# Computing the expert gates of a vision tower inside its second attention, and storing the normalised rows beside the balancing

## The reference, cut to what matters

```python
h = _layernorm(h + _L1_attn_ref(h, ...))     # causal attention in each image, 8 heads, mixed with a moving average
h = _layernorm(h + _L1_ffn_ref(h, gate_w, experts))

def _L1_ffn_ref(x, gate_w, experts):         # e = 8 experts
    gates = x @ gate_w                       # [64 images, 65 tokens, 8]
    cg = sinkhorn(gates)                     # 8 rounds: normalise over tokens, then over experts
    vals, idx = top_k(cg per expert, m)      # m = 65 // 8 = 8 rows per expert, of all 4160
    gate_values = (vals > 0.5)
    outputs = (x[idx] @ experts) * gate_values
    return (sum of the outputs that fell on a row) / (their count + 1)

def _layernorm(x, eps=1e-05):
    return (x - mean(x)) / sqrt(var(x) + eps)
```

## Time and profile before

| | us |
|---|---|
| median of 3 runs | 896.49 |
| the profiled execution | 896.61 |
| its span, first to last instruction | 894.8 |

### The profile page before, as it was taken

One profiled execution on the slowest core, in us unless ns is written; L12 is line 12 of the kernel. 1 busy time (PEld: TensorE's weight loads), 2 busy tenths in 40 slices (PEclk: granted clock), 3 DMA queues, 4 the chain that ended last, 5 costly groups with the idle time before them and its releaser, 6 DMA issues. The chain is left out here.

```text
span 894.8 us, 21478 instructions
## 1 busy us (share of the span) xinstructions
PE 655.1 (73%) x8452; PEld 529.1 (59%) x8452; DVE 526.6 (59%) x948; ACT 328.2 (37%) x774; POOL 245.0 (27%) x283
## 2 busy tenths in 40 slices
PE   2999999999999966507877787696877777455002
PEld 2888888888888854407625565585666566354001
DVE  0365666666655663362125778686778888333862
ACT  0113444434444443304422343433666767411000
POOL 0353334443333330000012233202443443252000
PEclk9999999999999976555698878555999999555555
DMA  8523343222222000159204300000000000033000
GB/s 330 214 111 120 139 158 127 108 108 108 108 108 108 2 2 1 45 147 155 42 0 51 46 0 0 1 0 2 2 2 0 0 1 3 1 98 94 24 1 4
DMA packets 32913, 57.45 MB, mean 64 GB/s; under 512 B 12370, under 2 KB 29954, under 8 KB 30370
## 3 DMA queue, kind: packets, MB, share of 16 engines
q1 hardware_dynamic: 32803, 56.74, 21.5%
q0 software_dynamic: 64, 0.07, 0.0%
HBM read 48.14 MB, written 8.66 MB: 63 GB/s over the span
## 5 line engine op out<-in xcount | busy, mean ns | idle before, releaser
L375 PE MATMUL a_bank<-a_x,a_tok_w 128*128 128x256 f32 (+1 forms) x608 | 150.4, 389 | 15.8 <-DVE a_ht L555 15.8
L375 PEld LDWEIGHTS a_bank<-a_x,a_tok_w 128*128 128x128 f32 (+1 forms) x608 | 113.0, 192 | 37.3 <-DMA tables<-in_tables 15.7
L124 POOL TENSOR_TENSOR a_qt<-a_qp,data 128x512 f32<-128x512 f32 x64 | 71.9, 1155 | 2.1 <-POOL a_qp L616 1.6
L616 POOL TENSOR_TENSOR a_qp<-a_rope 128x260 f32<-128x260 f32 x16 | 11.8, 734 | 177.2 <-DVE a_rope L499 177.2
L282 ACT ACTIVATE a_at<-a_bank 65x256 f32<-65x256 f32 x128 | 38.9, 390 | 25.9 <-PE a_bank L259 25.9
L1340 ACT ACTIVATE b_at<-b_bank 65x512 f32<-65x512 f32 x64 | 34.9, 601 | 36.5 <-PE b_bank L1214 36.5
L493 DVE SCALAR_TENSOR_TENSOR a_ht<-a_bank,data 128x256 f32<-128x256 f32 x16 | 7.7, 484 | 64.4 <-PE a_bank L375 64.4
L259 PE MATMUL a_bank<-a_mix,a_e 64*65 64x64 f32 x1024 | 40.6, 234 | 0.0
L1403 POOL TENSOR_TENSOR b_e<-b_e,b_inv 128x520 f32<-128x520 f32 (+1 forms) x32 | 35.5, 1110 | 13.8 <-DVE b_inv L1278 13.7
L259 PEld LDWEIGHTS a_bank<-a_mix,a_e 64*65 64x65 f32 x1024 | 36.0, 147 | 4.0 <-issue 3.4
L172 DVE TENSOR_REDUCE a_mx<-a_bank 128x6 f32<-128x390 f32 (+1 forms) x48 | 25.6, 534 | 21.1 <-PE a_bank L146 21.1
(11 more groups left out here) (241 smaller groups left out, 1536.0 us busy)
## 6 DMA issues: line engine op xcount, KB each, us to landing
a_x<-in_x SPq DMA_DIRECT2D x16, 2304.0 KB, 7.9
lag_rows<-r_kernel SPq DMA_DIRECT2D x1, 4192.5 KB, 39.4
lags<-lag_rows SPq DMA_DIRECT2D x1, 2112.5 KB
base<-places SPq DMA_DIRECT2D x1, 2080.0 KB
token_rows<-n_h SPq DMA_DIRECT2D x16, 130.0 KB
out<-n_plain SPq DMA_DIRECT2D x16, 130.0 KB
expert_weights<-in_w SPq DMA_DIRECT2D x2, 1024.0 KB, 5.8
a_tok_w<-in_tok_w SPq DMA_DIRECT2D x1, 1152.0 KB, 6.7
```

The costliest lines, as they stand in the source:

```text
L124: nc.gpsimd.tensor_tensor(qt[:, b * BLOCKS * P:(b + 1) * BLOCKS * P].rearrange("p (c h i) -> p c h i", i=qb, h=HEADS), wide(by_image[:, b, ...
L375: mm = nc.tensor.matmul(banks[0][:, 0:GP], w[0:rows, k * DIM:(k + 1) * DIM], x[p][0:rows, k * GP:(k + 1) * GP], start=(k == 0), stop=(k == ...
```

## The change

The gates are computed in the attention's loop from `z`, the row before its mean is subtracted and before it is scaled. The mean is taken out of the gate matrix instead (once, at the head of the block, with one matmul), and the scale `rstd` is multiplied into the 65x512 gates at the head of the last block. In the loop that adds, per group, four transposes and four matmuls on TensorE (each fp32 matmul shows as two records) and two copies on ScalarE; the mean's scaling moves from VectorE to ScalarE. `output` waits for the copy of the gates of the group before, since both share a bank.

The orders of the engines in that loop are rearranged: TensorE turns the last token's rows with the first half and makes the values before the second half; VectorE takes the first maxima ahead of the first subtraction, and `residual` and the row sums before both inversions; the last token's rows (`LAST`) are in the first part of the exponentials; ScalarE saves heads before it squares, and squares one group later.

`norm_and_gate` is gone. Its head stands in the last block, `norm_and_route`. ScalarE makes the plain rows with one instruction per image beside the balancing, and SyncE stores them. The table of `h3` rows is gone too: the 64 rows are gathered from the output, together with the standard deviations of the second norm by a second indirect DMA, and multiplied by them on VectorE.

```diff
-        LAST = PAIRS * UNIT
+        LAST = UNIT
+        FIRST = (0, UNIT + 1)
...
+        parts = [slice(0, UNIT + 1), slice(UNIT + 1, SLOTS)]
...
-                wait_past(pe, S.z_ready, g)
+                wait_past(pe, S.gates_saved, g)
...
+            def turn_rows(g):
+
+                pe.wait_ge(S.z_ready, g + 1)
+                for b in range(GI):
+                    mm = nc.tensor.transpose(ybank[:, b * TOKENS:(b + 1) * TOKENS], z[:, b, :], T("ident", TOKENS)[:, 0:TOKENS])
+                mm.then_inc(S.z_turned, 1)
+
+            def gates(g):
+                pe.wait_ge(S.zf_ready, g + 1)
+                for b in range(GI):
+                    mm = nc.tensor.matmul(gatebank[:, b * EXPERTS1:(b + 1) * EXPERTS1], zf[:, b * TOKENS:(b + 1) * TOKENS],
+                                          gate[:, :], start=True, stop=True)
+                mm.then_inc(S.gates_done, 1)
+
+            nc.tensor.matmul(banks[2][:, 0:EXPERTS1], T("mean"), D("gate1"), start=True, stop=True).then_inc(S.gate_mean, 1)
+            pe.wait_ge(S.gate_ready, 1)
...
                     turn_pair(g, p, 0)
+                    turn_last(g, p)
                 if exists(g + 2):
                     if exists(g + 1):

                         pe.wait_ge(S.masked, 2 * (g + 2))
                     queries_keys(g + 2)
+                if exists(g + 1):
+
+                    pe.wait_ge(S.masked, 2 * (g + 2))
+                    values(g + 1, 1 - p)
                 if exists(g):
-                    turn_last(g, p)
+                    pe.wait_ge(S.probs_ready, 2 * g + 2)

                     pe.wait_ge(S.at_ready, 5 * g + 2)
                     turn_pair(g, p, 1)
@@ -1238,14 +1264,14 @@
                     pe.wait_ge(S.v_ready, g + 1)
                     values_of_image(nc, 0, at, vs[p], obank)
                     values_of_image(nc, 1, at, vs[p], obank)
-                if exists(g + 1):
-
-                    pe.wait_ge(S.masked, 2 * (g + 2))
-                    values(g + 1, 1 - p)
+                if exists(g - 1):
+                    turn_rows(g - 1)
                 if exists(g):
                     pe.wait_ge(S.at_ready, 5 * g + 5)
                     values_of_image(nc, 2, at, vs[p], obank)
                     values_of_image(nc, 3, at, vs[p], obank).then_inc(S.av_done, 1)
+                if exists(g - 1):
+                    gates(g - 1)
...
-            def average(g):
+            def total_of_rows(g):
                 dve.wait_ge(S.z_ready, g + 1)
+
+                wait_past(dve, S.mean_scaled, g)
                 nc.vector.tensor_reduce(sums[:, :], z[:, :, :], AX.X, ALU.add).then_inc(S.sum_done, 1)
-                dve.wait_ge(S.sum_done, g + 1)
-                nc.vector.tensor_scalar(means[:, :], sums[:, :], 1.0 / DIM, None, ALU.mult).then_inc(S.mean_scaled, 1)

             nc.vector.tensor_scalar(parity_bias[:, :], T("parity"), D("bq1"), None, ALU.mult).then_inc(S.biased, 1)
+            dve.wait_ge(S.gate_mean, 1)
+            nc.vector.tensor_tensor(gate[:, :], D("gate1"), banks[2][:, 0:EXPERTS1], ALU.subtract).then_inc(S.gate_ready, 1)
...
+                    peaks(g + 1, 0, e[1 - p])
+                    peak_of_last(g + 1)
                     shift(g + 1, 0, e[1 - p])
                     shift_last(g + 1, e[1 - p])
+                    peaks(g + 1, 1, e[1 - p])
                     shift(g + 1, 1, e[1 - p])
                 if exists(g - 1):
                     residual(g - 1)
+                    total_of_rows(g - 1)
                 if exists(g + 1):
                     invert(g + 1, 0, e[1 - p])
-                if exists(g - 1):
-                    average(g - 1)
-                if exists(g + 1):
                     invert(g + 1, 1, e[1 - p])
...
+            def average(g):
+                act.wait_ge(S.sum_done, g + 1)
+
+                wait_past(act, S.centred, g)
+                nc.scalar.activation(means[:, :], sums[:, :], ACT.Copy, scale=1.0 / DIM).then_inc(S.mean_scaled, 1)
+
+            def save_rows(g):
+                act.wait_ge(S.z_turned, g + 1)
+
+                wait_past(act, S.gates_done, g)
+                nc.scalar.activation(zf[:, :], ybank[:, 0:GT], ACT.Copy, scale=SMALL).then_inc(S.zf_ready, 1)
+
             def squares(g):

                 act.wait_ge(S.centred, g + 1)
+                wait_past(act, S.squared, GI * g)
                 for b in range(GI):
                     nc.scalar.activation(sq[:, b, :], base[:, g, b, :], ACT.Square, scale=SMALL,
                                          accum_out=R.var[:, bass.ds(GI * g + b, 1)]).then_inc(S.squared, 1)

-            act.wait_ge(S.v_cleared, 2)
-            act.wait_ge(S.biased, 1)
-            for g, i, p in pipeline(act, 2, GROUPS + 1):
+            def save_gates(g):
+                act.wait_ge(S.gates_done, g + 1)
+                nc.scalar.activation(R.gates1[:, g, :], gatebank, ACT.Copy).then_inc(S.gates_saved, 1)
+
+            for g, i, p in pipeline(act, 2, GROUPS + 2):
                 if exists(g):
                     save_pair(g, 0)
+                    save_last(g)
                 if exists(g + 1):
                     exponent(g + 1, 0, e[1 - p])
                 if exists(g + 2):
                     queries_keys(g + 2)
                 if exists(g):
-                    save_last(g)
                     save_pair(g, 1)
                 if exists(g + 1):
+                    save_values(g + 1, 1 - p)
                     exponent(g + 1, 1, e[1 - p])
-                    save_values(g + 1, 1 - p)
-                if exists(g - 1):
-                    squares(g - 1)
+                if exists(g - 1):
+                    save_rows(g - 1)
+                    average(g - 1)
                 if exists(g):
                     save_heads(nc, act, g, obank, ot, S)
+                if exists(g - 1):
+                    save_gates(g - 1)
+                if exists(g - 2):
+                    squares(g - 2)
...
-def norm_and_gate(nc, A, R, out):
...
-def sinkhorn_and_route(nc, A, R, out):
+def norm_and_route(nc, A, R, out):
...
+            nc.vector.memset(eps[:, :], EPS * SMALL ** 2).then_inc(S.prepared, 1)
+            then(nc.vector.tensor_scalar(fin[:, :], R.var[:, :], OVERFLOW, None, ALU.is_le))
+            nc.vector.tensor_scalar(var[:, :], R.var[:, :], 1.0 / DIM, None, ALU.mult).then_inc(S.prepared, 1)
+            dve.wait_ge(S.roots, 1)
+            then(nc.vector.reciprocal(rstd[:, :], sd[:, :]))
+            dve.wait_ge(S.prepared, 2)
+            then(nc.vector.tensor_tensor(var[:, :], var[:, :], rstd[:, :], ALU.mult))
+            then(nc.vector.tensor_tensor(var[:, :], var[:, :], rstd[:, :], ALU.mult))
+            nc.vector.tensor_tensor(var[:, :], var[:, :], fin[:, :], ALU.mult).then_inc(S.prepared, 1)
+            then(nc.vector.tensor_tensor(rstd[:, :], rstd[:, :], fin[:, :], ALU.mult))
+            then(nc.vector.tensor_tensor(gates, gates, over_cols(rstd), ALU.mult))
+            dve.wait_ge(S.roots, 2)
+            then(nc.vector.reciprocal(rstd2[:, :], sd[:, :]))
+            nc.vector.scalar_tensor_tensor(out=rstd2[:, :], in0=rstd2[:, :], scalar=SMALL, in1=rstd[:, :],
+                                           op0=ALU.mult, op1=ALU.mult).then_inc(S.scales, 1)
+            then(nc.vector.tensor_scalar(gates, gates, 1e-10, None, ALU.max))
...
+            dve.wait_ge(S.got, 32)
+            nc.vector.tensor_scalar(x[:, :], norm[:, :], sd_x[:, :], None, ALU.mult).then_inc(S.rescaled, 1)
...
+            pe.wait_ge(S.roots, 2)
+            nc.tensor.transpose(banks[5][0:IMAGES, 0:TOKENS], sd[:, :], T("ident", TOKENS)[:, 0:TOKENS]).then_inc(S.root_turned, 1)
...
+            act.wait_ge(S.prepared, 2)
+            nc.scalar.activation(sd[:, :], var[:, :], ACT.Sqrt, bias=eps[:, :]).then_inc(S.roots, 1)
+            act.wait_ge(S.prepared, 3)
+            nc.scalar.activation(sd[:, :], var[:, :], ACT.Sqrt, bias=R.eps[0:TOKENS, :]).then_inc(S.roots, 1)
+            act.wait_ge(S.root_turned, 1)
+            nc.scalar.activation(sd_rows[:, :], banks[5][0:IMAGES, 0:TOKENS], ACT.Copy).then_inc(S.root_rows, 1)
+            act.wait_ge(S.scales, 1)
+            for i in steps(act, 0, GROUPS // 2):
+                for p in range(2):
+                    g = 2 * i + p
+
+                    wait_past(act, stored[p], 16 * i)
+                    for b in range(GI):
+                        nc.scalar.activation(plain[p][:, b, :], base[:, g, b, :], ACT.Copy,
+                                             scale=rstd2[:, bass.ds(GI * g + b, 1)]).then_inc(S.plain, 1)
...
+            sp.wait_ge(S.root_rows, 1)
+            sp.dma_start(R.roots.rearrange("(b t) n -> b (t n)", b=IMAGES), sd_rows[:, :]).then_inc(S.root_saved, 16)
+            for i in steps(sp, 0, GROUPS // 2):
+                for p in range(2):
+                    sp.wait_ge(S.plain, GI * (2 * i + p + 1))
+                    sp.dma_start(outs[2 * i + p], plain[p][:, :, :]).then_inc(stored[p], 16)
...
```

(11 more changed lines are left out.)

160 lines of the change are left out of this document (29 added, 131 removed).

## The result

The changed kernel took 864.86 us (median of 4, 863.68 to 866.16) against 897.75 us (894.71 to 899.91) for the kernel before: a ratio of 0.9634, 95% interval 0.9612 to 0.9656. It is faster, by 32.9 us where 45.8 had been forecast, and it lies outside the range of 843 to 859 us. In the table of experiments further down, one of e8's four executions is left out, which took 1244 us where the others took 846.7 to 849.2. The profiled spans are 894.8 and 864.0 us. Cut at the same marks, they differ as follows; "forecast" is the prediction's term for the stretch.

What follows compares the result with a forecast made beforehand. Bounds: ScalarE-TensorE hand-overs in the attention loop, the gate block, and the balancing-routing chain. Gate block -42.4, tail +1.45, loop -3.8, head +0.5, end -1.5 sum to -45.8 us from 896.6: 850.8 us, range 843 to 859.

Steps and rivals of the forecast that it cites:

- The loop: Second attention's 15 steps, first to sixteenth mask: shorter ring and fewer low-clock stretches, -3.8 us (ends -7 and +8).
- The ring: Chain of ScalarE and TensorE waits setting the attention loop's period: 9.2 us per group against 9.34, -2.1 us.
- the two half-won dips: Two low-clock stretches in the attention loop, costing 3.4 us together; half counted as won through shorter TensorE gaps, -1.7 us.
- D: Rival: new waits keep TensorE at 1.2 GHz through the attention loop, 13.5 us per group, 918 us; chance 0.03.
- B: Rival: TensorE's clock stays up through the attention's loop and end, 846 us; chance 0.17.
- A: Rival: new hand-overs through three engines slow the attention loop to 9.7 us per group, 860 us; chance 0.16.
- The two dips of the kernel before: Low-clock stretches in the old attention loop, priced at 3.4 us together from longer outputs and turnings.
- The end of the attention: After the last groups: less waiting for the head copy, less added transposes, copy and squares, -1.5 us (-4 to +1).
- The gate block: Between attention and balancing: first column sum 5.35 us after the root's table load instead of 47.8, -42.4 us.
- C: Rival: plain-row stores beside the balancing come late and hold up SyncE's list store, 856 us; chance 0.08.
- The tail: After routing: a second gather issued behind the first (+1.10) and a scaling with hand-over (+0.35), +1.45 us.
- The head: Start of the second attention: averaging and subtracting the gate matrix's mean delays the first queries, +0.5 us.

Runs made afterwards that it cites:

- e8: e1 plus five unread 128x256 matmuls in the last block while the gathers run: 846.88 us, ratio 0.9438.
- e2: Changed kernel with TensorE's values and ScalarE's copy of them put back at their old places: 863.87 us, ratio 0.9569.
- e1: Changed kernel plus, per group, two unread 128x124 matmuls before the second copies' wait and one 128x256 before the gates' wait: 849.53 us, ratio 0.9410.
- e5: Kernel before the change plus two unread 128x256 matmuls per group ahead of TensorE's longest wait: 896.78 us, ratio 1.0000.
- e4: Changed kernel with the four turnings of z's rows done as plain matmuls with the identity instead of transposes: 871.16 us, ratio 0.9646.
- e9: Changed kernel plus two unread 128x256 matmuls per group ahead of the gates only: 852.38 us, ratio 0.9520.
- e6: Changed kernel with e1's two places filled with five unread transposes each instead of matmuls: 850.32 us, ratio 0.9468.
- e7: Changed kernel plus only e1's first filling, two unread 128x124 matmuls per group before the second copies' wait: 860.90 us, ratio 0.9593.
- e3: Changed kernel without the gates' transposes, matmuls and copies in the loop, so its result is wrong: 840.74 us, ratio 0.9332.

## Why the prediction was right or wrong

**The loop, -3.8 forecast, +7.0 measured.** This is the step that failed. The failing sentence is "TensorE now has shorter gaps between its pieces, so I count half of that as won". The gaps did get shorter (from 640 to 750 us TensorE's longest was 1.17 us before and 0.61 after), and the level got worse: 15.8 us low before, 48.1 after. The ring itself was walked well. At the full level it was to be 9.2 us per group; e2 has 9.04 and 9.18 before its first fall, e1 8.9 to 9.3. With the two half-won dips the loop was to take 136.3 us; e1 has 133.3. To that comes what the level costs, 13.75 us (e1 against after): 133.3 + 13.75 = 147.1. Where it goes on the ring is in the rows: scores 1.29 for 0.91, the last token's 0.45 for 0.32, output 1.97 for 1.09, 1.4 us together. From the start of the scores to ScalarE's next copies it is 4.28 us (690.68 to 694.96), in e1 2.90. The groups are 10.2 us long in the mean against 9.1 in e1, so a small part of it is taken back elsewhere.

I had the mechanism among the rivals, but only in one size: D had TensorE at the lower level through the whole loop, 13.5 us per group, 918 us, and got 0.03. A fall in a third of each group was in none of them, and it made 864.9 us of a forecast 850.8. B, the level staying up everywhere, was priced at 846, which is 0.944 of the 896.6 before; that is e1, at 0.941. A's time, 860, was the nearest, but by another mechanism, new hand-overs in series; the hand-overs are there (0.43 and 0.61 us of waiting in the loop), but with the clock up the loop with them is at the 9.0 to 9.2 us of e2, not at A's 9.7.

The two dips of the kernel before were overpriced, too: 3.4 us by adding up longer instructions, where their two intervals are 2.3 us shorter in e5. There was a third, at 623.4 us, that the prediction didn't count.

**The end of the attention, -1.5 forecast, +0.4 measured.** The same cause, as far as the runs show. The last outputs alternate between the levels in the kernel after. e1, where all three are at the full one (1.09, 1.06 and 1.06 us), ends in 21.6 us instead of 24.99, that is, 3.0 better than before, twice the forecast; e4, with 1.97, 1.13 and 1.94, in 27.5.

```profile
763.57 1.97 PE L1201 MATMUL b_bank<-data,b_ot 128*65 128x128 f32 x8
771.81 1.17 PE L1201 MATMUL b_bank<-data,b_ot 128*65 128x128 f32 x8 [0.38 <-ACT gates L1409]
780.67 1.94 PE L1201 MATMUL b_bank<-data,b_ot 128*65 128x128 f32 x8 [0.37 <-ACT gates L1409]
```

**The gate block, -42.4 forecast, -42.7 measured.** Right, and with its parts. The head is 5.06 us where 5.35 was reckoned: the scaling of the gates is 0.69 us, beside the second root as said, and the clipping 0.41 for an assumed 0.5. The plain rows took 1.84 us per group (2.45 of work and 1.24 of waiting for each pair of groups) where 2.0 was assumed; the last stores left around 822 us and the list wasn't held. C is out.

**The tail, +1.45 forecast, +2.1 measured.** The two gathers were indeed issued one after the other, 1.10 us for the first, and the scaling is 0.28. Missing were 0.30 us between the two and 0.63 us more ahead of the first (1.07 us from the cast's start to the gather, 0.44 before), whose cause no run shows. The data of the second came 0.31 us sooner after its issue than the 2.62 us of the one gather of the earlier trace rows, by the chain that ended last:

```profile
848.62 2.31 DMA e_norm_rows<-out,e_take
```

The scaling with its hand-overs added 0.38 us (0.43 from that landing to the turning, 0.05 before). 0.63 + 1.10 + 0.30 - 0.31 + 0.38 = 2.1.

**The head, +0.5 forecast, +0.4 measured.** Right. The +1.8 us ahead of the attention, where no line was changed, had no term; e9 has its first mask at 613.97 and the kernel before at 614.44, and the other runs have it between 614.6 and 619.9, so it looks like the scatter of executions.

**The transposes.** The rule of the Trainium skill, "TensorE: Matmul & The Clock Gate", Part 4: PE-mode transpose, that the prediction left undecided would have moved the sum the right way, by 1.7 us, but for a reason that e6 speaks against; and in e4, with no added transposes, the level fell all the same.

**What stays open** is what makes the level fall. It isn't the idle time as such. The kernel before is less busy over 640 to 750 us, 85 of 110 us against 98.6, and has 0.97 there, with its last fall in the loop at 660.9 us. (Part of the 98.6 is that work takes longer at the lower level; in the stretches at the full level TensorE is busy for 85% of the time after and 76% before.) It has whole windows with almost nothing in them, at 1.00 throughout:

```profile
693.00:694.00 1.00, 0.12 (x5) 0.00 (x0) 1.00 (x3) 1.00 (x3) 0.16 (x1) 1.00 0.00 0
...
698.00:699.00 1.00, 0.06 (x4) 0.00 (x0) 0.78 (x2) 0.91 (x6) 0.68 (x2) 1.00 0.00 0
```

The falls of the kernel after come at the pace of its groups, one in each, and a fall lengthens the group that it is in; that the two hold each other up is a guess that fits e7, where no group is spared after the first fall. It wasn't tested. What the traces add is that the falls lie 10.24 us apart in e2, e4 and e7 too, although the work in their groups differs, and that the groups settle at 10.2 to 10.3 us in the mean in all four. So as long as the level falls once per group, the period says little about the length of the ring, and that e2 and e4 have the loop of the kernel after doesn't show that their edits are free at the full level.

## What to carry over

When a change reshapes TensorE's work in a loop, price the clock as a term of its own, with a case in which it falls once per pass: here it was worth some 17 us in loop and end, more than all other terms but one, and shorter gaps were no protection. If the level falls in every pass, unread matmuls or transposes put ahead of TensorE's short waits, about as long as these, brought it back here: ratio 0.9634 to 0.941, the lowest of the kernels that compute the gates. Check it first in the granted clock over the loop, since in a loop that holds its level (e5) the same filling gives nothing.

## What the runs showed of the hardware that was not expected

- A less busy loop mostly kept its level and a busier one lost it in each group: 77% busy at a mean granted clock of 0.97, 90% at 0.83, with no gap over 0.61 us.
- One fall of 3.4 us to the lower level costs about 1.15 us of a group of this loop (e3: 9.11 us against 7.96).
- Transposes of fp32 among matmuls keep the level up: 12.7 us low instead of 48.1.
- Turning four 65x128 pieces by plain fp32 matmuls takes 1.11 us as eight records, by transposes 0.46 us as four.
- 4.63 us of matmuls after 15.78 us of idling did not bring the level back for the experts' matmuls (3.58 us with and without).
- A second indirect gather is issued 1.40 us after the first, and lands 2.31 us after its start.
